# Experts of a sparse feed-forward block: tiles of 128 rows against 544 slots per expert in two column phases

## The chip, the cores and the metric

The kernel runs on one core of one Trainium2 chip. The metric is device time in microseconds, the median of three runs. TensorE is written PE in the profile (PEld for its weight loads), VectorE DVE, ScalarE ACT, GpSimd POOL, SyncE SP.

## The reference

The input x has 4 images of 512 channels on 16 x 32 positions. A layer norm over channels, a causal depthwise convolution along the channel axis with 3, 7 and 15 taps, a 96-to-32 mixing and a residual come first. The change is in what follows, on 2048 tokens of 512 features:

```python
t = _to_tokens(x)                       # 2048 tokens x 512
xn = _ln_t(t)
probs = softmax(xn @ gate_w.T)          # 8 experts
topk_w, topk_idx = top_k(probs, 2); topk_w /= topk_w.sum(-1)
h = silu(xn @ w1[e]) * (xn @ w3[e])     # 512 -> 1024, every expert e
y = h @ w2[e]                           # 1024 -> 512
t = t + sum_e y_e * full_w[:, e]
```

The kernel computes each expert only for the tokens that chose it, 4096 pairs of token and expert. The result must hold float32 accuracy, so each product of matrices is made from a high part (float32r, written hi) and a low part (lo, the rest): hi x hi, lo x hi and hi x lo, three matmuls.

## The kernel before

**Ahead of the experts.** The convolution stage ends with the normalised tokens in DRAM (xn_rows), the gate logits, and the residual sums in the output. DVE finds two experts per token, ranks tokens within each expert and builds one-hot matrices; slots(0) and slots(1) (L671) multiply them, and bank 5 then holds the token number of each slot, 16 columns of 128 slots per expert. From it come src_i (what to gather), dst_i (where to add) and gate_i (which gate).

**Tiles.** An expert's slots are worked in tiles of 128 rows, only as many as its tokens need; DVE computes a table of live tiles (tile_expert, tile_last, tile_col), and every engine runs a loop over up to 39 tiles with values loaded from it. 36 tiles are live here.

**One tile on TensorE** (pe_tile). The stationary operand is always 128 x 128 of the rows (xT_hi, xT_lo, hT_hi, hT_lo), the moving one 512 columns of weights. up(k) for four units of w1 and w3 is 4 x 12 products; turn_h transposes h (L734), turn_tokens the next tile's gathered rows (L712), 12 transposes together; down sums 24 products into bank 7. ACT applies silu (L559), makes high parts (L563, L572) and writes y scaled by the gate (L580). DVE multiplies (L1042) and makes low parts (L1046, L1019).

**Weights.** Each expert has six units of 128 x 2048 (1 MB). SP loads unit k of the next expert when its low half is made; ACT makes the high half (high_half, L265), DVE the low half (low_half, L270), POOL that of unit 1. This is done in an expert's last tile.

**POOL's queue** (pool_tile) is strictly in program order. In a tile it gathers the rows of the tile after next, as soon as xg is free (after turn_tokens), and then waits for y:

```python
next_expert(1)
pool.wait_ge(xg_ps, t2)                       # gather, L404
...
pool.wait_ge(y_out, t1)                       # then y's rows: add_at, gate_at
pool.indirect_dma_start(out=out, ..., in_=y[:], compute_op=ALU.add)   # L438
gather_gates(gate_at[:, 0:1])                 # L410
```

y is one buffer: ACT waits for the add to have landed (y_st) before it writes the next. SP waits at L333 until all adds have landed.

**Columns of the rows.** In a row such as `437.00 0.18 POOL L428 COPY gather_at<-src_i`, the first number is the start in us from the span's start, the second the length.

Of the kernel before, what the change touches and what calls it, by code (L numbers as in the profile page):

```python
# [6 lines left out]
F32R = mybir.dt.float32r  # L7
I32 = mybir.dt.int32
ALU = mybir.AluOpType
# [20 lines left out]
TILES = NT * 2 + E - 1  # L30
SLOT_TILES = 2 * -(-(TILES + 2) // 2)
# [9 lines left out]
GRID = TOKENS // P  # L41

# [67 lines left out]
def metaformer(nc, xt, taps_d, mix_d, joint_d, gate_d, units, out):  # L110

    with ExitStack() as ctx:
# [37 lines left out]
        xg = at("xg", XT_AT, [P, NQ, P])  # L150
        y = at("y", XT_AT + 2 * KB, [P, L])

        hT_hi = at("hT_hi", F_AT, [P, 2, 4, P], F32R)
        hT_lo = at("hT_lo", F_AT + 4 * KB, [P, 2, 4, P], F32R)
        xT_hi = at("xT_hi", F_AT + 8 * KB, [P, NQ, P], F32R)
        xT_lo = at("xT_lo", F_AT + 10 * KB, [P, NQ, P], F32R)
        h = at("h", F_AT + 12 * KB, [P, 2, 512])
        xnb = [at(f"xnb{n}", F_AT + 2 * KB * n, [P, NB, P]) for n in range(XB)]
        h_at = F_AT + 12 * KB
        over = at("over", h_at, [P, E, GRID])  # L160
        passed = at("passed", h_at + 512, [P, SLOT_TILES, E])
        te = at("te", h_at + 1856, [P, 4, SLOT_TILES])
        number, empty = (at(n, h_at + 2560 + 512 * k, [P, P]) for k, n in enumerate(("number", "empty")))
# [3 lines left out]
        def keep(name, shape, dt=F32):  # L167

            size = 4
            for n in shape[1:]:  # L170
# [17 lines left out]
        slot_gate = keep("slot_gate", [P, SLOT_TILES])  # L188
        gather_at = keep("gather_at", [P, 1], I32)
        add_at = keep("add_at", [P, 1], I32)  # L190
        gate_at = keep("gate_at", [P, 1], I32)
        gate_row = keep("gate_row", [P, 1])
        tile_col = keep("tile_col", [1, SLOT_TILES], I32)
        tile_expert = keep("tile_expert", [1, TILES], I32)
        tile_last = keep("tile_last", [1, TILES], I32)
        all_tiles = keep("all_tiles", [1, 1], I32)
# [49 lines left out]
        gates_made, gate_st, gate_index, gate_land = (sem("gates_made"), sem("gate_st"), sem("gate_index"),  # L246
                                                      sem("gate_land"))
        xn_half, scanned = sem("xn_half"), sem("scanned")
        src_ready, tables_ready, gate_ready = sem("src_ready"), sem("tables_ready"), sem("gate_ready")
# [3 lines left out]
        xg_in, xg_ps, xT_hi_out, xT_lo_out = sem("xg_in"), sem("xg_ps"), sem("xT_hi_out"), sem("xT_lo_out")  # L253
        unit_done = sem("unit_done")
        silu_out, h_out, hT_ps, hT_hi_out, hT_lo_out = (sem("silu_out"), sem("h_out"), sem("hT_ps"),
                                                        sem("hT_hi_out"), sem("hT_lo_out"))
        y_out, y_st = sem("y_out"), sem("y_st")
# [17 lines left out]
        def _(sp):  # L275
# [54 lines left out]
            sp.wait_ge(tables_ready, 1)  # L330
            total = sp.value_load(all_tiles[0:1, 0:1], min_val=E, max_val=TILES)
            sp.wait_ge(y_st, total * 16)
# [3 lines left out]
        def _(pool):  # L336
# [65 lines left out]
            def gather(index):  # L402

                pool.indirect_dma_start(  # L404
                    out=xg[:].rearrange("p q i -> p (q i)"), out_offset=None, in_=xn_dram,
                    in_offset=bass.IndirectOffsetOnAxis(ap=index, axis=0)).then_inc(xg_in, 16)

            def gather_gates(index):

                pool.indirect_dma_start(  # L410
                    out=gate_row[:], out_offset=None, in_=gate_dram,
                    in_offset=bass.IndirectOffsetOnAxis(ap=index, axis=0)).then_inc(gate_land, 16)

            def column(t):
                return pool.value_load(tile_col[0:1, bass.ds(t, 1)], min_val=0, max_val=P - 1)

            def pool_tile(t, t1, t2, following):

                last = pool.value_load(tile_last[0:1, bass.ds(t, 1)], min_val=0, max_val=1)

                def next_expert(k):

                    with pool.If_ne(last.val, 0):
                        low_half(pool, following, k)

                next_expert(1)
                pool.wait_ge(xg_ps, t2)
                pool.tensor_copy(gather_at[:], src_i[:, bass.ds(column(t2), 1)]).then_inc(gather_index, 1)  # L428
                pool.wait_ge(xn_st[XB - 1], 16 * NT // XB)
                pool.wait_ge(gather_index, t2)  # L430
                gather(gather_at[:, 0:1])

                pool.wait_ge(y_out, t1)
                pool.tensor_copy(add_at[:], dst_i[:, bass.ds(column(t), 1)]).then_inc(add_index, 1)  # L434
                pool.tensor_copy(gate_at[:], gate_i[:, bass.ds(column(t1), 1)]).then_inc(gate_index, 1)  # L435
                pool.wait_ge(spare_st, 16)
                pool.wait_ge(add_index, t1)
                pool.indirect_dma_start(  # L438
                    out=out, out_offset=bass.IndirectOffsetOnAxis(ap=add_at[:, 0:1], axis=0),
                    in_=y[:], in_offset=None, compute_op=ALU.add).then_inc(y_st, 16)  # L440
                pool.wait_ge(gate_st, 16)
                pool.wait_ge(gate_index, t1)
                gather_gates(gate_at[:, 0:1])
# [6 lines left out]
            gather(src_i[:, 0:1])  # L450
            pool.wait_ge(tables_ready, 1)
            pool.wait_ge(gate_st, 16)
            gather_gates(gate_i[:, 0:1])
            pool.wait_ge(xg_ps, 1)
            pool.tensor_copy(gather_at[:], src_i[:, bass.ds(column(1), 1)]).then_inc(gather_index, 1)
            pool.wait_ge(gather_index, 1)
            gather(gather_at[:, 0:1])
            pool_tile(0, 1, 2, 1)
            with pool.Fori(1, TILES) as t:
                live = pool.value_load(tile_expert[0:1, bass.ds(t, 1)], min_val=0, max_val=E)  # L460
                with pool.If_ne(live.val, 0):
                    pool_tile(t, pool.snap(t + 1), pool.snap(t + 2), live)
                    pool.nop()

        @block.scalar
        def _(act):
# [69 lines left out]
            for k in range(3):  # L536
                high_half(act, 0, k)

            act.wait_ge(ex_in, 1)
            act.activation(ex[:], ex[:], ACT.Exp).then_inc(ex_out, 1)  # L540

            act.wait_ge(xg_ps, 1)
            act.activation(xT_hi[:], B[6][:].rearrange("p (q i) -> p q i", i=P), ACT.Copy).then_inc(xT_hi_out, 1)
            for k in range(3, UNITS):
                high_half(act, 0, k)

            def act_tile(t, following):
                last = act.value_load(tile_last[0:1, bass.ds(t, 1)], min_val=0, max_val=1)

                def next_expert(*ks):  # L550

                    with act.If_ne(last.val, 0):
                        for k in ks:
                            act.wait_ge(unit_done, t * UNITS + (k + 1))
                            high_half(act, following, k)

                def silu(j):
                    act.wait_ge(unit_done, t * UNITS + (2 * j + 1))
                    act.activation(h[:, j, :], B[2 * j][:], ACT.Silu).then_inc(silu_out, 1)  # L559

                def hi(j):
                    act.wait_ge(hT_ps, t * 2 + (j + 1))
                    act.activation(hT_hi[:, j, :, :], B[4 + j][:].rearrange("p (c n) -> p c n", n=P),  # L563
                                   ACT.Copy).then_inc(hT_hi_out, 1)

                silu(0)
                next_expert(0, 1)
                silu(1)
                hi(0)
                next_expert(2)  # L570
                act.wait_ge(xg_ps, t + 2)
                act.activation(xT_hi[:], B[6][:].rearrange("p (q i) -> p q i", i=P),  # L572
                               ACT.Copy).then_inc(xT_hi_out, 1)
                hi(1)
                next_expert(3, 4)
                act.wait_ge(unit_done, t * UNITS + UNITS)
                act.wait_ge(gate_ready, t + 1)
                if not isinstance(t, int):
                    act.wait_ge(y_st, t * 16)
                act.activation(y[:].rearrange("p (q i) -> p q i", i=P), B[7][:].rearrange("p (i q) -> p q i", q=NQ),  # L580
                               ACT.Copy, scale=slot_gate[:, bass.ds(t, 1)]).then_inc(y_out, 1)

                next_expert(5)

            act.wait_ge(tables_ready, 1)
            act_tile(0, 1)
            with act.Fori(1, TILES) as t:
                live = act.value_load(tile_expert[0:1, bass.ds(t, 1)], min_val=0, max_val=E)
# [545 lines left out]
```

## Time and profile before

| | |
|---|---|
| three runs | 847.27, 848.59, 849.71 us, median 848.59 |
| profiled execution | 847.05 us, of it span 845.4 us |
| PE / DVE / ACT / POOL busy | 94 / 42 / 38 / 32% |
| granted TensorE clock, mean over the span | 0.97 |
| chain that ended last | PE 86%, DVE 7%, DMA 2% |

The chain of work that ended last is followed back from the last instruction; 86% of it is TensorE. TensorE's busy time comes from modelled ends of pipelined matmuls, so intervals between starts say more than lengths do.

### The profile page before, as it was taken

How to read it: one execution, taken by the hardware profiler on the slowest of the kernel's cores; microseconds unless marked ns; L12 is line 12 of the kernel's file. 1: busy time of each engine (PE TensorE's matmuls, PEld its weight loads, DVE VectorE, ACT ScalarE, POOL GpSimd, SP SyncE). 2: the span in 40 equal slices, each digit the busy share in tenths (PEclk: the TensorE clock that was granted, in tenths of full speed). 3: DMA queues.
4: the chain of work that ended last, by engine and by line, in shares of the span. 5: the costliest groups of instructions: out<-in, count | busy, mean ns of one | idle time of the engine just before them, and what ended most of it. 6: DMA issues, size and time to landing. Idle time of an engine off the chain costs nothing.

```text
span 845.4 us, 13004 instructions
## 1 busy us (share of the span) xinstructions
PE 791.5 (94%) x3764; PEld 655.6 (78%) x3765; DVE 351.7 (42%) x791; ACT 318.6 (38%) x487; POOL 268.8 (32%) x313
## 2 busy tenths in 40 slices
PE   4999999628999999999999999999999999999993
PEld 3777888527888888888888888888888888888882
DVE  5886758685113621172216223511361172244111
ACT  6784755432214512262127125311441262262120
POOL 4346210003233422361216315322341262243311
PEclk9999999659999999999999999999999999999997
DMA  7247678628111811173116513712281164111111
GB/s 237 47 75 138 150 162 175 256 105 326 25 31 34 317 39 25 27 263 95 32 30 201 159 25 88 271 25 37 46 302 37 25 224 136 25 37 25 30 32 25
DMA packets 55873, 91.72 MB, mean 108 GB/s; under 512 B 7344, under 2 KB 40496, under 8 KB 49712
## 3 DMA queue, kind: packets, MB, share of 16 engines
q1 hardware_dynamic: 45728, 71.64, 27.2%
q0 software_dynamic: 9408, 19.42, 12.0%
q10 hardware_dynamic: 720, 0.46, 0.2%
q8 instruction: 7, 0.11, 0.1%
q14 instruction: 10, 0.08, 0.0%
HBM read 64.97 MB, written 18.15 MB: 98 GB/s over the span
## 4 chain that ended last, share of the span: by engine, by line
PE 86%; DVE 7%; DMA 2%; issue 2%; ACT 1%; POOL 0%; POOLq 0%; ACTq 0%; DVEq 0%
PE bank L720 23%; PE bank L718 23%; PE bank L719 23%; PE bank L734 4%; PE bank L631 3%; PE bank L632 3%; PE bank L633 3%; PE bank L712 2%; PE bank L653 1%; DMA xg<-xn_rows,gather_at 1%; DVE bn L782 1%; DVE wc_lo L823 1%; PE bank L671 1%; PE bank L646 1%; DVE mv L791 1%
## 5 line engine op out<-in xcount | busy, mean ns | idle before, releaser
L718 PE MATMUL bank<-w_hi,xT_hi 128*128 128x512 f32 x576 | 229.0, 398 | 4.3 <-DVE xT_lo L1019 4.3
L720 PE MATMUL bank<-w_hi,xT_lo 128*128 128x512 f32 x576 | 225.9, 392 | 0.0
L719 PE MATMUL bank<-w_lo,xT_hi 128*128 128x512 f32 x576 | 225.2, 391 | 0.0
L1042 DVE TENSOR_TENSOR h<-bank,h 128x512 f32<-128x512 f32 x72 | 49.8, 692 | 294.0 <-PE bank L720 293.8
L718 PEld LDWEIGHTS bank<-w_hi,xT_hi 128*128 128x128 f32 x576 | 108.9, 189 | 26.3 <-DVE xT_lo L1019 4.7
L720 PEld LDWEIGHTS bank<-w_hi,xT_lo 128*128 128x128 f32 x576 | 108.7, 189 | 23.4
L719 PEld LDWEIGHTS bank<-w_lo,xT_hi 128*128 128x128 f32 x576 | 108.9, 189 | 21.8
L718 PE MATMUL bank<-w_hi,hT_hi 128*128 128x512 f32 x288 | 118.7, 412 | 0.0
L559 ACT ACTIVATE h<-bank 128x512 f32<-128x512 f32 x72 | 43.1, 599 | 197.4 <-PE bank L720 197.4
L720 PE MATMUL bank<-w_hi,hT_lo 128*128 128x512 f32 x288 | 112.6, 391 | 0.0
L719 PE MATMUL bank<-w_lo,hT_hi 128*128 128x512 f32 x288 | 112.3, 390 | 0.0
L1046 DVE TENSOR_TENSOR hT_lo<-bank,hT_hi 128x512 fp32r<-128x512 f32 x72 | 49.8, 692 | 112.7 <-ACT hT_hi L563 112.7
L265 ACT ACTIVATE w_hi<-w_raw 128x2048 fp32r<-128x2048 f32 x48 | 90.8, 1911 | 8.4 <-DMA w_raw<-in_units 6.2
L270 DVE TENSOR_TENSOR w_lo<-w_raw,w_hi 128x2048 fp32r<-128x2048 f32 x41 | 91.6, 2282 | 0.0
L580 ACT ACTIVATE y<-bank,slot_gate 128x512 f32<-128x512 f32 x36 | 24.8, 690 | 134.0 <-PE bank L720 134.0
L434 POOL COPY add_at<-dst_i 128x1 int32 x36 | 16.0, 444 | 177.5 <-ACT y L580 177.5
L372 POOL TENSOR_TENSOR wc<-taps,mixT 128x256 f32<-128x256 f32 (+4 forms) x48 | 41.7, 888 | 74.5 <-DVE wc_lo L823 71.8
L438 POOL DMA_INDIRECT out_x<-y,add_at x36 | 58.5, 1625 | 19.5 <-POOL gate_at L435 17.8
L720 PEld LDWEIGHTS bank<-w_hi,hT_lo 128*128 128x128 f32 x288 | 54.1, 188 | 11.8
L719 PEld LDWEIGHTS bank<-w_lo,hT_hi 128*128 128x128 f32 x288 | 54.4, 189 | 8.7
L631 PE MATMUL bank<-xs_parts,wc_hi 128*128 128x512 f32 x128 | 54.8, 428 | 6.6 <-DVE xs_parts L817 6.6
L718 PEld LDWEIGHTS bank<-w_hi,hT_hi 128*128 128x128 f32 x288 | 54.2, 188 | 8.6
(145 smaller groups left out, 924.2 us busy)
## 6 DMA issues: line engine op xcount, KB each, us to landing
w_raw<-in_units SPq DMA_DIRECT2D x48, 1024.0 KB, 5.9
joint<-xs_parts SPq DMA_DIRECT2D x64, 128.0 KB, 3.8
out_x<-XT SPq DMA_DIRECT2D x17, 256.0 KB, 3.6
XT<-in_x SPq DMA_DIRECT2D x16, 256.0 KB, 7.0
xn_rows<-xnb SPq DMA_DIRECT2D x16, 256.0 KB, 2.5
xg<-xn_rows,gather_at POOLq DMA_INDIRECT x37, 3.4
out_x<-y,add_at POOLq DMA_INDIRECT x36
gate_row<-gate_rows,gate_at POOLq DMA_INDIRECT x36
```

The costliest lines, as they stand in the source:

```text
L265: eng.activation(w_hi[k][:], w_raw[k][:], ACT.Copy).then_inc(hi_ready[k], 1)
L270: eng.tensor_tensor(w_lo[k][:], w_raw[k][:], w_hi[k][:], ALU.subtract).then_inc(lo_ready[k], 1)
L372: ins = pool.tensor_tensor(wc[t % WB][:, at_col:at_col + count * P].rearrange("p (a d q) -> p a d q", d=D, q=NQ), lags.rearrange("p (a q) ...
L438: pool.indirect_dma_start(out=out, out_offset=bass.IndirectOffsetOnAxis(ap=add_at[:, 0:1], axis=0), in_=y[:], in_offset=None, compute_op=A ...
L559: act.activation(h[:, j, :], B[2 * j][:], ACT.Silu).then_inc(silu_out, 1)
L631: pe.matmul(out_bank, wc_hi[t % WB][:, cols], hi, start=first, stop=False)
L718: pe.matmul(B[bank][:], stat_hi, hi, start=start, stop=False)
L719: pe.matmul(B[bank][:], stat_hi, lo, start=False, stop=False)
L720: return pe.matmul(B[bank][:], stat_lo, hi, start=False, stop=stop)
L734: ins = pe.transpose(B[4 + j][:, P * c:P * c + P], h[:, j, P * c:P * c + P], ident[:])
L1042: dve.tensor_tensor(h[:, j, :], B[2 * j + 1][:], h[:, j, :], ALU.mult).then_inc(h_out, 1)
L1046: dve.tensor_tensor(hT_lo[:, j, :, :], B[4 + j][:].rearrange("p (c n) -> p c n", n=P), hT_hi[:, j, :, :], ALU.subtract).then_inc(hT_lo_out, 1)
```

## The change

The loop over tiles goes. Each expert has 4 x 128 + 32 = 544 slots (ROOM), worked without conditions in two phases: wide, with 128 + 128 + 32 = 288 slots, and even, with 128 + 128 = 256. Expert 0 and expert 7 are written out, 1 to 6 are a loop. A loop for leftover tiles of experts with more than 544 tokens stands at the end (rest_live, rest_expert, rest_col).

- First products (up): the weights are stationary, 128 x 128 of them, and the slots' columns move, 288 or 256. A chunk c of eight is 128 hidden features, 24 products into two banks. h comes out already transposed, and turn_h is gone.
- ACT and DVE work per chunk on 288 or 256 columns: silu, product, high part, low part.
- Second products (down_rows): the rows stay stationary, 512 columns of w2 move, one sum per tile: three sums after the wide phase (128, 128 and 32 rows), two after the even one. w2's columns are laid out in another order on the host.
- Two buffers for gathered rows, five for gates; y stays one buffer.
- The gather of tile 3 stands first in pool_expert, that of tile 4 next; then tiles 0 and 1 of the next expert, then the adds.
- POOL makes no low halves any more. DVE's table of leftovers, slot tables and gates move into expert 0. count(1) runs ahead of slots(0); all six high halves of expert 0 are made ahead of its x.

```diff
+ROOM = 4 * P + P // 4
+WIDE, EVEN = 2 * P + P // 4, 2 * P
+TILE = ((0, 0, 0, P), (1, 0, P, P), (4, 0, 2 * P, P // 4), (2, 1, 0, P), (3, 1, P, P))
...
+            def gather_tile(column, m, buffer, turned, nth):
+
+                pool.wait_ge(xt_ps, nth)
+                pool.wait_ge(xt_ps, turned)
+                pool.tensor_copy(gather_at[buffer][:], src_i[:, bass.ds(pool.snap(column), 1)]).then_inc(gather_index, 1)
+                pool.wait_ge(src_ready, 1)
+                pool.wait_ge(gather_index, nth)
+                gather(xg[buffer][0:m], gather_at[buffer][0:m, 0:1], xg_in[buffer])
+
+            def add_rows(column, m, nth):
+
+                pool.wait_ge(y_out, nth)
+                pool.tensor_copy(add_at[:], dst_i[:, bass.ds(pool.snap(column), 1)]).then_inc(add_index, 1)
...
+            def pool_expert(e, first=False, last=False):
+
+                def gather_next(j, buffer, ahead, turned, nth):
+                    gather_tile(e * GRID + (GRID * ahead + TILE[j][0]), TILE[j][3], buffer, e * 5 + turned, e * 5 + nth)
+
+                def add(j):
+                    add_rows(e * GRID + TILE[j][0], TILE[j][3], e * 5 + (j + 1))
+                    if not last:
+                        next_gates(j, e * GRID + (GRID + TILE[j][0]), e * 5 + (j + 1))
+
+                gather_next(3, 1, 0, 2, 1)
+                gather_next(4, 0, 0, 3, 2)
...
+                if not last:
+                    gather_next(0, 0, 1, 5, 3)
+                    gather_next(1, 1, 1, 5, 4)
+                for j in range(3):
+                    add(j)
+                if not last:
+                    gather_next(2, 0, 1, 6, 5)
+                for j in range(3, len(TILE)):
+                    add(j)
...
+            def chunk(c, n, cols, opening=False):
+                act.wait_ge(up_ps, n(c + 1))
+                if not opening:
+                    act.wait_ge(hT_lo_out, n(c - 1))
+                act.activation(hs[c % 2][:, 0:cols], B[2 * (c % 2)][:, 0:cols], ACT.Silu).then_inc(silu_out, 1)
+                act.wait_ge(h_out, n(c + 1))
+                act.activation(hT_hi[:, c, 0:cols], hs[c % 2][:, 0:cols], ACT.Copy).then_inc(hT_hi_out, 1)
+
+            def rows_out(j, bank, m, nth, gates, opening=False):
+                act.wait_ge(y_ps, nth + 1)
+                act.wait_ge(gate_land[j], gates)
+                if not opening:
+                    act.wait_ge(y_st, nth * 16)
+                act.activation(y[0:m], B[bank][0:m, :], ACT.Copy, scale=slot_gate[0:m, j:j + 1]).then_inc(y_out, 1)
...
+                for j, bank in enumerate((4, 6, 7)):
+                    tile_rows(j, bank)
+                for c in range(HC):
+                    chunk(c, even, EVEN)
+                    if c in (1, 3, 5) and not last:
+                        x_high(c // 2, 5, e * 5 + (6 + c // 2))
+                    if c in (4, 6) and not last:
+                        if c == 4:
+                            act.wait_ge(up_ps, even(4))
+                        high_half(act, e + 1, (c - 4) // 2)
+                if not last:
+                    act.wait_ge(up_ps, even(8))
+                    high_half(act, e + 1, 2)
+                    high_half(act, e + 1, 3)
+                tile_rows(3, 4)
+                tile_rows(4, 6)
...
+            def up(c, n, cols, i, split, opening=False):
...
+                if not opening:
+                    pe.wait_ge(h_out, n(c - 1))
+                at_col = slice(P * (c % 4), P * (c % 4) + P)
+                for m in range(2):
+                    k, hidden = c // 4 * 2 + m, B[2 * (c % 2) + m][:, 0:cols]
+                    for a in range(NQ):
+                        x_hi, x_lo = xT_hi[i][:, a, 0:cols], xT_lo[i][:, a, 0:cols]
+                        pe.matmul(hidden, w_hi[k][:, a, at_col], x_hi, start=(a == 0), stop=False)
+                        pe.matmul(hidden, w_lo[k][:, a, at_col], x_hi, start=False, stop=False)
+                        ins = pe.matmul(hidden, w_hi[k][:, a, at_col], x_lo, start=False, stop=(a == NQ - 1))
+                ins.then_inc(up_ps, 1)
+
+            def down_waits(c, n, split):
+
+                if c % 4 == 0:
+                    pe.wait_ge(lo_ready[4 + c // 4], split)
+                if c == 0:
+                    pe.wait_ge(hT_lo_out, n(HC - 1))
+                if c == HC - 1:
+                    pe.wait_ge(hT_lo_out, n(HC))
+
+            def down_rows(first, bank, n, split, m=P):
+
+                for c in range(HC):
+                    down_waits(c, n, split)
+                    k, a = 4 + c // 4, c % 4
+                    hi, lo = hT_hi[:, c, first:first + m], hT_lo[:, c, first:first + m]
+                    pe.matmul(B[bank][0:m, :], hi, w_hi[k][:, a, :], start=(c == 0), stop=False)
+                    pe.matmul(B[bank][0:m, :], hi, w_lo[k][:, a, :], start=False, stop=False)
+                    ins = pe.matmul(B[bank][0:m, :], lo, w_hi[k][:, a, :], start=False, stop=(c == HC - 1))
+                ins.then_inc(y_ps, 1)
...
+                for c in range(HC):
+                    if c == 0:
+                        pe.wait_ge(xT_lo_out, e * 5 + 3)
+                    up(c, wide, WIDE, 0, split, first and c < 2)
+                    if c == 1:
+                        gathered(1, e * 32 + 32, 3)
+                        turn_x(xg[1], 5, P)
+                    if c == 4:
+                        gathered(0, e * 48 + 32, 4)
+                        turn_x(xg[0], 5, P)
...
+                for c in range(HC):
+                    if c == 0:
+                        pe.wait_ge(xT_lo_out, e * 5 + 5)
+                    if not last and c == 5:
+                        gathered(0, e * 48 + 64, 7)
+                    up(c, even, EVEN, 1, split)
...
+                for c in range(HC):
+                    chunk(c, even, EVEN)
+                    if c in (1, 3, 5) and not last:
+                        x_low_half(c // 2, 5, e * 5 + (6 + c // 2))
+                    if c in (5, 7) and not last:
+                        low_half(dve, e + 1, (c - 5) // 2)
+                if not last:
+                    low_half(dve, e + 1, 2)
+                    low_half(dve, e + 1, 3)
```

In the diff, functions with pool. stand on POOL, act. on ACT, pe. on TensorE, dve. on DVE; the last piece is dve_expert's even phase. The wait in gathered(1, ...) is for the landed gather of tile 3.

## Rows read from the trace of the kernel before

**Rows 1.** The page: the span, then busy time of each engine

```profile
span 845.4 us, 13004 instructions
...
PE 791.5 (94%) x3764; PEld 655.6 (78%) x3765; DVE 351.7 (42%) x791; ACT 318.6 (38%) x487; POOL 268.8 (32%) x313
```

**Rows 2.** Windows: stretch and length, busy time (count) by engine, granted clock, DMA

```profile
core 0: us, PE busy (x) PEld busy (x) DVE busy (x) ACT busy (x) POOL busy (x), PEclk, DMA share, GB/s
...
147.50:153.00 5.50, 3.33 (x28) 2.91 (x26) 3.79 (x17) 3.71 (x10) 0.00 (x0) 1.00 0.32 95
...
158.70:188.60 29.90, 11.31 (x51) 10.53 (x50) 24.35 (x78) 9.77 (x8) 1.14 (x1) 0.50 0.53 217
188.60:194.00 5.40, 5.33 (x13) 4.17 (x14) 5.30 (x7) 4.72 (x3) 0.19 (x1) 0.50 0.50 112
194.00:200.00 6.00, 6.00 (x30) 4.99 (x29) 5.15 (x4) 0.91 (x2) 5.13 (x3) 0.99 1.00 412
```

**Rows 3.** Timeline of TensorE's weight loads (PEld), at both clocks: start, length

```profile
189.69 0.33 PEld L718 LDWEIGHTS bank<-w_hi,xT_hi 128*128 128x128 f32 x1
...
190.12 0.33 PEld L719 LDWEIGHTS bank<-w_lo,xT_hi 128*128 128x128 f32 x1
...
264.42 0.19 PEld L718 LDWEIGHTS bank<-w_hi,xT_hi 128*128 128x128 f32 x1
...
269.86 0.19 PEld L718 LDWEIGHTS bank<-w_hi,xT_hi 128*128 128x128 f32 x1
```

**Rows 4.** Timeline of TensorE around four transposes of h

```profile
272.35 0.19 PEld L720 LDWEIGHTS bank<-w_hi,xT_lo 128*128 128x128 f32 x1
...
272.81 0.60 PE L734 MATMUL bank<-ident,h 128*128 128x128 f32 x4
...
273.48 0.19 PEld L720 LDWEIGHTS bank<-w_hi,xT_lo 128*128 128x128 f32 x1
```

**Rows 5.** Groups of instructions: count, busy us, mean ns, idle before and its releaser

```profile
L718 PE MATMUL bank<-w_hi,xT_hi 128*128 128x512 f32 x576 | 229.0, 398 | 4.3 <-DVE xT_lo L1019 4.3
...
L718 PE MATMUL bank<-w_hi,hT_hi 128*128 128x512 f32 x288 | 118.7, 412 | 0.0
...
L270 DVE TENSOR_TENSOR w_lo<-w_raw,w_hi 128x2048 fp32r<-128x2048 f32 x41 | 91.6, 2282 | 0.0
L265 ACT ACTIVATE w_hi<-w_raw 128x2048 fp32r<-128x2048 f32 x48 | 90.8, 1911 | 8.4 <-DMA w_raw<-in_units 6.2 <-PE bank L720 2.2
...
L559 ACT ACTIVATE h<-bank 128x512 f32<-128x512 f32 x72 | 43.1, 599 | 197.4 <-PE bank L720 197.4
```

**Rows 6.** Timeline from the first gather to the first product

```profile
179.64 1.14 POOL L404 DMA_INDIRECT xg<-xn_rows,src_i  x1 [51.66 <-DVE src_i L975]
...
188.67 0.79 PE L718 MATMUL bank<-w_hi,xT_hi 128*128 128x512 f32 x1 [4.29 <-DVE xT_lo L1019]
```

**Rows 7.** Timeline of the end: last product, y, its rows added

```profile
831.90 0.39 PE L720 MATMUL bank<-w_hi,hT_lo 128*128 128x512 f32 x1
832.57 0.69 ACT L580 ACTIVATE y<-bank,slot_gate 128x512 f32<-128x512 f32 x1 [4.44 <-PE bank L720]
...
835.56 1.62 POOL L438 DMA_INDIRECT out_x<-y,add_at  x1 [0.60 <-POOL gate_at L435]
```

**Rows 8.** SP's last wait, which ends when all rows are added: last start

```profile
L333 SPq EVENT_SEMAPHORE  x1: 17/17/17, 840.2 to 840.2; - x1
```

**Rows 9.** Timeline of POOL, one gather of token rows

```profile
437.00 0.18 POOL L428 COPY gather_at<-src_i 128x1 int32 x1 [6.38 <-PE bank L712]
437.94 0.97 POOL L404 DMA_INDIRECT xg<-xn_rows,gather_at  x1 [0.76 <-POOL gather_at L428]
```

**Rows 10.** Timeline: a gather's issue on POOL while DVE makes weight halves

```profile
191.87 6.69 DVE L270 TENSOR_TENSOR w_lo<-w_raw,w_hi 128x2048 fp32r<-128x2048 f32 x3
...
196.66 2.74 POOL L404 DMA_INDIRECT xg<-xn_rows,gather_at  x1 [0.27 <-POOL gather_at L455]
```

**Rows 11.** Gathers of token rows, all 38: from issue to landing

```profile
DMA to landing us min/median/max: 3.1/3.4/8.3
```

More of the change, by code:

```diff
@@ L29 @@
 E = 8
-TILES = NT * 2 + E - 1
-SLOT_TILES = 2 * -(-(TILES + 2) // 2)
 UNITS = 6
@@ L400, in _, with gather @@
                 multiply_taps(t)
[L402 removed]
+            def gather(out_rows, index, landed):
                 pool.indirect_dma_start(
[L405 to L408 removed]
+                    out=out_rows.rearrange("p q i -> p (q i)"), out_offset=None, in_=xn_dram,
+                    in_offset=bass.IndirectOffsetOnAxis(ap=index, axis=0)).then_inc(landed, 16)
@@ L410, in gather_gates @@
+            def gather_gates(j, index):
+                m = TILE[j][3]
                 pool.indirect_dma_start(
[L411 to L435, printed above, removed]
@@ L534, in _ @@
                     wc_high(t + 2)
-            for k in range(3):
+            for k in range(UNITS):
                 high_half(act, 0, k)
[L539 to L572, printed above, removed]
-                               ACT.Copy).then_inc(xT_hi_out, 1)
[L574 to L583, printed above, removed]
@@ new lines, in _ @@
+            pe.wait_ge(src_ready, 2)
+            pe.wait_ge(xg_in[0], 16)
+            turn_x(xg[0], 5, P)
+            pe.wait_ge(xg_in[1], 16)
+            turn_x(xg[1], 4, P)
+            pe.wait_ge(xg_first, 16)
+            turn_x(y_rows, 6, P // 4)
+            pe_expert(0, first=True)
+            with pe.Fori(1, E - 1) as e:
+                pe_expert(e)
+            pe_expert(E - 1, last=True)
+            pe.wait_ge(rest_ready, 1)
+            total = pe.value_load(all_rest[0:1, 0:1], min_val=0, max_val=REST)
@@ L982, in _ @@
-            then_next(dve.tensor_tensor(upto[:], upto_e[:], ntile[:].unsqueeze(1).broadcast_to([P, E, E]), ALU.mult))
-            then_next(dve.tensor_reduce(end[:], upto[:], AX_X, ALU.add))
-            slots_by_e = [1, SLOT_TILES, E]
-            ends = end[0:1, :].unsqueeze(1).broadcast_to(slots_by_e)
-            expert, live, following, column = (te[0:1, k, :] for k in range(4))
-            then_next(dve.tensor_tensor(passed[0:1], iota[0:1, 0:SLOT_TILES].unsqueeze(2).broadcast_to(slots_by_e),
-                                        ends, ALU.is_ge))
@@ new lines, in dve_expert, with wide, even @@
+            def dve_expert(e, first=False, last=False):
+                def wide(c):
+                    return e * 16 + c
+                def even(c):
+                    return e * 16 + (8 + c)
+                for c in range(HC):
+                    chunk(c, wide, WIDE)
+                    if first and c < 2:
+                        low_half(dve, 0, 2 + c)
+                    if c == 1:
+                        x_low_half(3, 5, e * 5 + 4)
+                    if first and c == 2:
+                        gate_shifts()
+                        slot_tables()
+                    if first and c == 3:
+                        make_gates()
+                    if c == 4:
+                        x_low_half(4, 5, e * 5 + 5)
+                    if c in ((4, 5) if first else (1, 3)):
+                        low_half(dve, e, 4 + (c - 4 if first else c // 2))
+                    if first and c == 6:
+                        rest_tables()
+                for c in range(HC):
+                    chunk(c, even, EVEN)
[6 more added lines that the diff above has]
+                    low_half(dve, e + 1, 3)
@@ new lines, in _ @@
+            for j, bank in enumerate((5, 4, 6)):
+                x_low_half(j, bank, j + 1)
+            dve_expert(0, first=True)
+            with dve.Fori(1, E - 1) as e:
+                dve_expert(e)
+            dve_expert(E - 1, last=True)
+            dve.wait_ge(rest_ready, 1)
+            everything = dve.value_load(all_rest[0:1, 0:1], min_val=0, max_val=REST)
+            with dve.If_ne(everything.val, 0):
+                with dve.Fori(0, REST) as r:
+                    live = dve.value_load(rest_live[0:1, bass.ds(r, 1)], min_val=0, max_val=1)
+                    with dve.If_ne(live.val, 0):
+                        x_low_half(0, 5, r + (E * len(TILE) + 1))
+                        for k in range(UNITS):
+                            low_half(dve, r + E, k)
+                        for c in range(HC):
+                            chunk(c, lambda k: r * 8 + (16 * E + k), P)
+                        dve.nop()
```

405 lines of the change are left out of this document (226 added, 179 removed).

## The prediction, made before the run

> **What bounds the kernel now.** Three views. The page gives a span of 845.4 us with TensorE busy for 94% of it [rows 1]; the execution took 847.05 us, 1.5 under the median of 848.59. The windows split it [rows 2]: until 158.7 the convolution, until 188.6 a thin stretch at half clock with TensorE busy for 11 of 30 us, then the experts with it always busy. The experts begin at 188.67 [rows 6] and their last product starts at 831.90 [rows 7], 643.4 us with its own 0.23. The timeline prices a product: its load and its 512 columns come every (269.86 - 264.42)/24 = 0.227 us at full clock, 0.43 at half [rows 3]. The reader is to see 512 columns at 2.4 GHz, 0.213, plus 0.014. Around four transposes three products take 1.13 us instead of 0.68 [rows 4]: 0.45 for four, 0.11 for a pair of load and 128 columns, twice what 128 columns need. So a load alone costs about 0.11, hidden under 512 columns and not under 128. Counting: 3 x 576 first and 3 x 288 second products [rows 5], 2592 in all, by 0.227 are 588.4, and 36 tiles with 12 transposes are 108 groups by 0.45, 48.6. Together 637.0 of 643.4; half clock until 194.0 [rows 2] explains 2.5 of the rest. The stage is TensorE's stream, without waits. What the change does to that stream, and to what it waits for, decides.
>
> **The stream after.** The reference's own inputs give 487 to 534 tokens per expert, so all fit in 544 slots and the tail for leftovers stays empty. First products: per expert 192 with 288 columns and 192 with 256. Second products: five sums by 24, 120 with 512 columns; the sum for 32 rows costs as much as one for 128. Columns are the same as before: 8 x (192 x 544 + 120 x 512) = 1,327,104 = 2592 x 512. The transposes of h go; those of x are 40 groups of four, 40 x 0.45 = 18.0. The gain is 30.6 us of transposes; the loss is that 2592 products become 8 x 504 = 4032 shorter ones. What a pair costs at 288 and 256 columns no row shows. Below: the larger of the columns (0.120, 0.107) and a load (about 0.11), so 0.120 and 0.108. With the 0.014 of rows 3 as a fixed part per pair: 0.1335 and 0.1202; with it in proportion, 0.1276 and 0.1134. Worse is possible, since load and columns are now equally long: I bound it by 0.150 for both, half way from the columns alone to load plus columns. I take the middle of fixed and proportional, 0.1305 and 0.117. Stream: 1536 x 0.1305 + 1536 x 0.117 + 960 x 0.227 + 18.0 = 200.4 + 179.7 + 217.9 + 18.0 = 616.0, that is 21 less than 637.0.
>
> The Trainium skill ("TensorE: Matmul & The Clock Gate", Back-to-back issue gap) gives N/2.4 + 2.5 ns per product at full clock, 0.1225 and 0.109 here; by it the sum below would end near 886. Its LDWEIGHTS section gives columns/1.2, 107 ns for 128: that agrees with the 0.11 of rows 4 and speaks against 256 columns, which no longer cover a load with anything to spare. At 512 columns its first rule gives 0.216 where rows 3 show 0.227, so I hold to the rows.
>
> **The new wait.** The order on POOL matters most. pool_expert(e) begins with the gather of tile 3 of its own expert, behind the last add and the last gate gather of expert e-1 in program order. TensorE wants this tile after two chunks of the wide phase. Before, the gather stood ahead of y's add and had a whole tile of some 17 us. From F, the first even second product:
>
> - TensorE: two sums, 48 x 0.227 = 10.9, then two chunks, 48 x 0.1305 = 6.3. It asks at F+17.2.
> - Tile 3's sum ends at F+5.4; ACT starts y 0.67 after the last product's start [rows 7], F+5.9, but two high halves of 1.91 [rows 5] stand before it, until about F+6.5. y is written by F+7.2.
> - POOL: copy 0.2, then 0.76 to the DMA instruction [rows 9]: F+8.4. DVE makes three low halves of 2.28 [rows 5] in F+3.1 to F+9.9, and a POOL issue beside such work took 2.74 instead of 0.97 [rows 10]. The add lands 4.6 after issue if undisturbed (835.56 to 840.2 [rows 7, 8]); here the next weights load at once, and a gather landed in up to 8.3 instead of 3.4 [rows 11] while the DMA share was 1.00 [rows 2]. I take 7: F+15.4.
> - y is one buffer, so tile 4's y waits for that landing: F+16.3 written. Copy and issue: F+17.4; 1.62 for the add [rows 7]; copy, 0.76, 0.99 for the gates: F+21.0; copy and 0.76: the gather issues at F+22.1 and lands 3.4 later [rows 11], F+25.5.
>
> TensorE waits 8.3 us in each of seven experts (the first has its gather early): 58. Without DVE's and the loads' disturbance and the high halves it is 5.2, so 36; with all of them in full 9.9, so 69. Nothing can be gained here.
>
> After such a gap the clock is likely low. In rows 2 it was granted in full until 153.0, though work thinned from 147.5, was half by 153, and came back only 5.4 us into the dense work of 188.6. 5.4 us at half clock give 5.4 x (1 - 0.1305/0.24) = 2.5 less work: seven times 17, from 0 (no fall) to 24.
>
> **Smaller terms.** The even second products wait for h's low part of chunk 6, which stands on DVE behind a low half of 2.28 begun after chunk 5: about 0.7 late, seven times 5 (0 to 10). The tile-2 gather of the next expert is asked for after five even chunks and lands at about the same time, cost 0 to 1 each; it is late next if products are quicker. Chunks: silu 0.4, product 0.4, copy 0.4, low part 0.4, estimates from 0.60 for 512 columns on ACT [rows 5], lie inside the 3.1 and 2.8 us of TensorE's next chunk. Gate and table arithmetic on DVE moves from before the first product into expert 0, with two table switches on ACT: hidden mostly, 1 us. What it frees at the start is used up: three gathers 1.4 apart from 179.64 [rows 6] land the last at 186.1, and turning and splitting it ends near 188.3, so the first product starts as now. count(1) ahead of slots(0) fills an idle stretch. POOL's low halves go to DVE, beside slack. The end: y 4 waits 0.7 for y 3, while POOL saves a column load and a copy, 0.
>
> **Sum.** 616.0 + 6.4 of other time as now + 58 + 17 + 5 + 1 = 703.4 against 643.4: 60 more. 847.05 + 60 = 907.
>
> **Rivals.**
> - *Faster.* The gather is in time. For it: POOL is busy only 32% [rows 1], and the gather's operands are ready a phase earlier. Against: POOL's program order puts it behind y of tile 4, which exists only at F+11 even without any wait, and rows 7, 9 and 11 leave at least 0.2 + 0.76 + 1.62 + 1.9 + 1.0 + 3.4 = 8.9 behind it. It decides if the landing comes before F+17.2, 8.3 earlier than I sum. Time: 907 - 58 - 17 = 832.
> - *The clock stays up* through the gaps: 907 - 17 = 890. For it: in rows 2 it held through 5.5 us with TensorE busy for 3.3. Against: here the gap is empty and longer.
> - *Pairs at their lower bound*: only the 6 wide and 8 even chunks outside the gap count, (144 x 0.0105 + 192 x 0.009) x 8 = 26 less: 881.
> - *Loads not hidden*, 0.150: (144 x 0.0195 + 192 x 0.033) x 8 = 73 more: 980.
> - *The change does not do what it says*: an expert over 544 tokens would reload all weights for a leftover tile. The counts exclude it.
>
> **How the numbers follow.** My forecast 57%, clock kept 18%, lower bound 12%, loads not hidden 5%, faster 7%, no change 1%. What a measurement can tell from no change is about 0.3%, 2.5 us. Faster 0.07, same 0.02, slower 0.91. The forecast's own range, gap 36 to 69, clock 0 to 24, pairs -26 to +8, mostly independent: 880 to 934. The range 868 to 938 leaves out the faster case and the unhidden loads, and takes in two favourable bounds together.
>
> **What would show it.** Per expert from 2 to 8, one idle stretch of 5 to 10 us on TensorE, ended by the gather of tile 3, after the second wide chunk, and half clock behind it; weight loads every 0.13 and 0.12 us in the first products; an execution of even second products that starts some 0.7 us late. Wrong would be: no such stretch (then 832), a pair over 0.14, or a second wait of the same size, above all ACT held by y in front of the even chunks, or the tile-2 gather.

## The result, and the profile after

The changed kernel takes 913.11 us, median of 4 runs (912.6 to 914.46), the kernel before 847.93 beside it: 7.69% slower, ratio 1.0769, interval 1.0746 to 1.0792. The profiled execution has a span of 911.0 us. The forecast was 907, with a range of 868 to 938.

The page of the changed kernel: span, busy time by engine, granted clock in 40 slices, the chain that ended last.

```profile
span 911.0 us, 13256 instructions
...
PE 797.7 (88%) x4928; PEld 711.1 (78%) x4929; DVE 373.6 (41%) x876; ACT 337.5 (37%) x607; POOL 233.8 (26%) x318
...
PEclk9999998579997999799979997999799979998997
...
PE 70%; DMA 10%; DVE 8%; issue 5%; POOL 4%; ACT 3%; POOLq 0%; ACTq 0%; DVEq 0%
```

Against [rows 1] TensorE's busy time has grown by 6 us and its share has fallen from 94 to 88%: the time came as waiting. The clock row has a dip in every fourth slice from the 13th to the 37th, which the kernel before had nowhere in its expert stage, and the chain holds 10% of DMA where it held 2%.

Who waited for whom, on TensorE in the expert stage: total us, times, longest.

```profile
PE bank L785 <- DMA xg<-xn_rows,gather_at: 62.1, 7, 9.8
...
PE bank L820 <- DVE hT_lo L1172: 1.1, 1, 1.1
```

Seven stretches, one for each expert from the second on, all ended by a gather. L785 is turn_x. The next rows are windows of one of them, the second expert's: start:end and length, busy time (count) by engine, granted clock, DMA.

```profile
core 0: us, PE busy (x) PEld busy (x) DVE busy (x) ACT busy (x) POOL busy (x), PEclk, DMA share, GB/s
259.00:270.00 11.00, 11.00 (x50) 8.91 (x49) 7.46 (x5) 5.76 (x6) 3.33 (x3) 1.00 0.66 258
270.00:276.50 6.50, 6.50 (x50) 6.44 (x48) 0.02 (x1) 0.99 (x2) 1.19 (x2) 1.00 0.72 226
276.50:285.00 8.50, 0.22 (x2) 0.00 (x0) 1.81 (x4) 2.98 (x4) 5.21 (x7) 0.73 0.34 62
285.00:290.50 5.50, 5.38 (x23) 5.39 (x24) 2.89 (x2) 0.60 (x1) 0.00 (x0) 0.50 0.17 51
290.50:297.60 7.10, 7.10 (x55) 7.10 (x54) 2.91 (x5) 3.52 (x5) 0.00 (x0) 0.99 0.40 148
```

The even second products (259.0 to 270.2), two wide chunks, then 8.5 us of nothing, then 5.5 us at half clock. (A PEclk of 0.73 or 0.69 is a mean over a stretch in which the clock went from full to half.) These windows are the forecast's F to F+38. What lies in the gap is read from the chain that ended last, in order of time, over the same stretch (start, length, what; TensorE's own pieces and the short ones between are left out):

```profile
264.80 0.70 ACT y L602
265.55 0.31 POOL add_at L439
265.90 0.76 issue
266.66 8.69 DMA out_x<-y,add_at
275.46 0.70 ACT y L602
276.21 0.20 POOL add_at L439
276.45 0.75 issue
277.20 1.61 POOL out_x L442
278.81 0.21 POOL gate_at L449
279.06 0.49 issue
279.91 0.88 issue
280.78 0.23 POOL gather_at L431
281.06 0.50 issue
281.76 3.31 DMA xg<-xn_rows,gather_at
```

With F = 259.02 this is the chain of the forecast step by step: y of tile 3 at F+5.8 (5.9 without the high halves, 6.5 with them forecast), its add issued at F+7.6 (8.4), landed at F+16.3 (15.4), tile 4's add issued at F+18.2 (17.4), the gather at F+22.7 (22.1), landed at F+26.1 (25.5). TensorE's last product before it starts at F+17.4, so by the spacing TensorE asks at F+17.5 (17.2).

This stretch is not like the other six. The same chain in the third expert's (F = 348.78) and in the eighth's (F = 800.21), and between them what DVE did in the third's:

```profile
355.48 2.34 POOL add_at L439
358.63 7.24 DMA out_x<-y,add_at
...
351.08 6.69 DVE L273 TENSOR_TENSOR w_lo<-w_raw,w_hi 128x2048 fp32r<-128x2048 f32 x3
...
810.06 4.92 DMA out_x<-y,add_at
```

In experts 3 to 8 POOL's copy of one column into add_at takes 2.34 instead of 0.31, and it ends 0.05 behind the last of DVE's three low halves. So the add is issued at F+9.8 (8.4 forecast), and tile 4's y starts at F+16.9 to F+17.7 in experts 3 to 7. In the eighth, which has no next weights to load, the add lands in 4.92 and y starts at F+14.8. By the starts, the stretches are 8.6, 9.3, 10.0, 9.4, 9.7, 9.3 and 7.0 us.

The products themselves, as weight loads of the changed kernel: start, length, line.

```profile
290.59 0.19 PEld L802 LDWEIGHTS bank<-xT_lo,w_hi 128*128 128x128 f32 x1
...
291.92 0.19 PEld L800 LDWEIGHTS bank<-xT_hi,w_hi 128*128 128x128 f32 x1
...
246.87 0.19 PEld L800 LDWEIGHTS bank<-xT_hi,w_hi 128*128 128x128 f32 x1
...
252.48 0.19 PEld L802 LDWEIGHTS bank<-xT_lo,w_hi 128*128 128x128 f32 x1
```

Ten loads in 1.33 us in the wide phase, 0.133 each; 47 in 5.61 in the even one, 0.119. That is columns plus 0.013 in both, the fixed form of the 0.014 of [rows 3].

### The profile page after: what moved, and what is told of

Same layout as the page of the kernel before. It is cut to its first block, busy times and chain, and to the rows that moved or that the text cites. A ratio compares the mean times of both kernels' runs of the same rounds, so it can differ in the third digit from the quotient of the medians.

```text
span 911.0 us, 13256 instructions
## 1 busy us (share of the span) xinstructions
PE 797.7 (88%) x4928; PEld 711.1 (78%) x4929; DVE 373.6 (41%) x876; ACT 337.5 (37%) x607; POOL 233.8 (26%) x318
## 4 chain that ended last, share of the span: by engine, by line
PE 70%; DMA 10%; DVE 8%; issue 5%; POOL 4%; ACT 3%; POOLq 0%; ACTq 0%; DVEq 0%
PE bank L800 13%; PE bank L801 12%; PE bank L802 12%; PE bank L820 7%; PE bank L822 7%; PE bank L821 6%; DMA out_x<-y,add_at 6%; PE bank L705 3%; DMA xg<-xn_rows,gather_at 3%; PE bank L706 2%; PE bank L707 2%; PE bank L785 2%; POOL add_at L439 2%; POOL out_x L442 1%; PE bank L727 1%
## 5 line engine op out<-in xcount | busy, mean ns | idle before, releaser
L800 PE MATMUL bank<-xT_hi,w_hi 128*128 128x256 f32 (+1 forms) x1024 | 306.3, 299 | 1.0 <-DVE xT_lo L1164 1.0
L801 PE MATMUL bank<-xT_hi,w_lo 128*128 128x256 f32 (+1 forms) x1024 | 302.0, 295 | 0.0
L802 PE MATMUL bank<-xT_lo,w_hi 128*128 128x256 f32 (+1 forms) x1024 | 301.3, 294 | 0.0
L800 PEld LDWEIGHTS bank<-xT_hi,w_hi 128*128 128x128 f32 x1024 | 200.2, 196 | 2.7 <-DVE xT_lo L1164 1.2
L801 PEld LDWEIGHTS bank<-xT_hi,w_lo 128*128 128x128 f32 x1024 | 200.0, 195 | 0.6
L802 PEld LDWEIGHTS bank<-xT_lo,w_hi 128*128 128x128 f32 x1024 | 199.8, 195 | 0.0
L820 PE MATMUL bank<-w_hi,hT_hi 128*128 128x512 f32 (+1 forms) x320 | 126.6, 396 | 1.3 <-DVE hT_lo L1172 1.1
L822 PE MATMUL bank<-w_hi,hT_lo 128*128 128x512 f32 (+1 forms) x320 | 125.9, 394 | 0.0
L821 PE MATMUL bank<-w_lo,hT_hi 128*128 128x512 f32 (+1 forms) x320 | 125.5, 392 | 0.0
L785 PE MATMUL bank<-ident,xg 128*128 128x128 f32 (+1 forms) x156 | 26.8, 301 | 68.8 <-DMA xg<-xn_rows,gather_at 62.1
L1172 DVE TENSOR_TENSOR hT_lo<-hs,hT_hi 128x256 fp32r<-128x256 f32 (+1 forms) x128 | 56.6, 443 | 63.7 <-ACT hT_hi L595 63.2
L785 PEld LDWEIGHTS bank<-ident,xg 128*128 128x128 f32 (+1 forms) x156 | 19.6, 157 | 71.9 <-DMA xg<-xn_rows,gather_at 56.7
```

The lines of the kernel that those rows point to most:

```text
L785: ins = pe.transpose(B[bank][:, m * q:m * q + m], buffer[0:m, q, :], ident[0:m, 0:m])
L800: pe.matmul(hidden, w_hi[k][:, a, at_col], x_hi, start=(a == 0), stop=False)
L801: pe.matmul(hidden, w_lo[k][:, a, at_col], x_hi, start=False, stop=False)
L802: ins = pe.matmul(hidden, w_hi[k][:, a, at_col], x_lo, start=False, stop=(a == NQ - 1))
L820: pe.matmul(B[bank][0:m, :], hi, w_hi[k][:, a, :], start=(c == 0), stop=False)
L821: pe.matmul(B[bank][0:m, :], hi, w_lo[k][:, a, :], start=False, stop=False)
```

## The experiments

Seven kernels. Each is the changed kernel with the edit shown, unless said otherwise. A period is the time from one expert's even second products to the next's, by the timeline; in the changed kernel it is 90.2 us on average over the first six.

**The early gathers.**

```diff
             def pool_expert(e, first=False, last=False):
...
-                gather_next(3, 1, 0, 2, 1)
-                gather_next(4, 0, 0, 3, 2)
                 if first:
+                    gather_next(3, 1, 0, 2, 1)
+                    gather_next(4, 0, 0, 3, 2)
...
                     gather_next(2, 0, 1, 6, 5)
+                    gather_next(3, 1, 1, 7, 6)
+                    gather_next(4, 0, 1, 8, 7)
                 for j in range(3, len(TILE)):
```

> The changed kernel with one move on POOL: the gathers of tiles 3 and 4 of the next expert are issued behind that of its tile 2, ahead of the last two adds, as soon as TensorE has turned what lay in their buffers. Theory (the wait is POOL's program order): the seven idle stretches of 6.9 to 9.8 us on TensorE, 62 in all, go, and with them the seven falls of the clock, 5.4 us of dense work at half clock each, worth 2.4 each, 17 in all. 913 - 62 - 17 = 834 us, against 848 for the kernel before. Rival A: a wait just behind takes the place (ACT held by y's add in front of the even chunks, or the gather of tile 4): some stretches of 2 to 5 us stay and the time is 850 to 880. Rival B: the stretches come from the gather itself, slow in the DMA queues: they stay at 8 us, 913.

846.88 us, ratio to the kernel before 0.999 (0.9981 to 1.0). The gather waits are gone from the list, the clock stays full from 191 us to the end, and the period is 80.6. 66 of the 79 expected us came back. The rest is rival A in small: a new entry in the waits on TensorE, and ACT's timeline beside it.

```profile
PE bank L802 <- DVE hs L1171: 8.3, 12, 1.0
```

```profile
276.08 0.69 ACT L604 ACTIVATE y<-bank,slot_gate 128x512 f32<-128x512 f32 x1 [10.98 <-DMA out_x<-y,add_at]
276.66 0.40 ACT L595 ACTIVATE hs<-bank 128x288 f32<-128x288 f32 x1
277.59 0.44 ACT L597 ACTIVATE hT_hi<-hs 128x288 fp32r<-128x288 f32 x1 [0.52 <-DVE hs L1171]
277.94 1.90 ACT L268 ACTIVATE w_hi<-w_raw 128x2048 fp32r<-128x2048 f32 x1
```

ACT stood 10.98 us before y of tile 4, until tile 3's rows had landed, and only then made the silu of the first wide chunk, which TensorE's third chunk needs. Two stretches near 1 us each, 1.9 by the starts, in each of the experts 2 to 7. The eighth has none: there tile 3's rows landed earlier, with no loads beside them. The sum expected below for both edits together counts seven times 2.0; six times 1.9 are 11.5 us.

**Filler on TensorE.**

```diff
                     if c == 1:
+                        if not first:
+                            for _ in range(38):
+                                pe.matmul(B[7][:], w_hi[0][:, 0, 0:P], w_hi[0][:, 1, :], start=True, stop=True)
                         gathered(1, e * 32 + 32, 3)
```

> The changed kernel with 38 added products of 512 columns into bank 7 (free then) on TensorE after the second wide chunk of experts 2 to 8, ahead of its wait for tile 3; nothing reads them. They take 38 x 0.227 = 8.6 us, about as long as the idle stretch, and do no useful work. Theory (the fall of the clock costs 17 us by itself): the clock stays full in the expert stage, the stretch is filled, and the time is 896, from 893 to 900. Rival: the clock costs nothing that the pipeline doesn't get back: 913 or more, since the filler overshoots the gather in the shortest stretch (6.9) by 1.7.

902.75 us (899.47 to 902.9), ratio 1.0648 (1.063 to 1.0666), 10.4 under the changed kernel, where 893 to 900 was expected; the profiled execution, the fastest of the four, has a span 13.4 under it. A window through the filler and one behind it:

```profile
270.00:290.00 20.00, 19.77 (x117) 17.54 (x116) 3.37 (x6) 4.58 (x7) 7.63 (x11) 1.00 0.51 144
290.00:360.00 70.00, 70.00 (x460) 62.65 (x459) 26.75 (x38) 24.61 (x41) 16.47 (x21) 1.00 0.31 95
```

Behind the stretch, the four transposes of tile 3 and the third to fifth chunk, from the first start to the last: first in the changed kernel, then with the filler.

```profile
285.12 1.11 PE L785 MATMUL bank<-ident,xg 128*128 128x128 f32 x4 [8.40 <-DMA xg<-xn_rows,gather_at]
...
297.52 0.29 PE L802 MATMUL bank<-xT_lo,w_hi 128*128 128x288 f32 x1
...
287.14 0.66 PE L785 MATMUL bank<-ident,xg 128*128 128x128 f32 x4 [0.23 <-DMA xg<-xn_rows,gather_at]
...
297.08 0.30 PE L802 MATMUL bank<-xT_lo,w_hi 128*128 128x288 f32 x1
```

The clock is 1.00 throughout and the period is 87.8, 2.4 shorter with TensorE doing 38 useless products in it. Not all of the 2.4 is the clock. The same work behind the stretch takes 12.4 us in the changed kernel and 9.9 with the filler; over the seven stretches the difference is between 1.7 and 2.6, 14.9 in all, 2.1 on average. The stretches themselves, from the product ahead to the first transpose, sum to 64.2 us in both kernels. So the fall of the clock has a price of its own, 14.9 us, where 17 was expected. The profile closes with it: the first expert's even second products, ahead of any filler, begin 1.5 us later (0.6 of it ahead of the stage), and 14.9 - 1.5 is the 13.4. Why they do, and why the three other executions took 3 us more than the profiled one, isn't settled.

**Two buffers for y.**

```diff
+        y = [at("y0", xg_at + 4 * KB, [P, L]), at("y1", hs_at + 8 * WIDE, [P, L])]
...
             def rows_out(j, bank, m, nth, gates, opening=False, waits=(), b=0):
...
-                if not opening:
-                    act.wait_ge(y_st, nth * 16)
-                act.activation(y[0:m], B[bank][0:m, :], ...)
+                for buffer, landed in waits:
+                    act.wait_ge(y_st[buffer], landed * 16)
+                act.activation(y[b][0:m], B[bank][0:m, :], ...)
```

Tile 0 still waits for all adds, since a token may be in two experts; add_at is doubled too.

> The changed kernel with two buffers for y (and for add_at), each with its own semaphore of landed adds: the y of tile 4 no longer waits for the rows of tile 3 to have landed. The order on POOL is as in the changed kernel. By the chain from the first even second product (F): y of tile 4 is written at F+12.0 instead of F+17.1, its add issues at F+13.4, behind the gates of tile 3, instead of F+18.2, the gather lands at F+21.3 instead of F+26.1. Theory: each stretch is 4.8 us shorter, 3.8 instead of 8.6: 34 less, 879; if the clock no longer falls in them, 17 less again, 862. Rival (y's single buffer is not in the chain; POOL is simply late with its queue): no change, 913.

880.02 us, ratio 1.0379 (1.0362 to 1.0396), 33 less. Waits on TensorE, and windows from the third expert:

```profile
PE bank L795 <- DMA xg<-xn_rows,gather_at: 34.6, 7, 5.3
```

```profile
361.50:366.50 5.00, 0.02 (x1) 0.00 (x0) 0.92 (x2) 0.91 (x3) 3.19 (x5) 1.00 0.36 83
366.50:372.00 5.50, 5.30 (x29) 5.30 (x30) 2.89 (x2) 0.60 (x1) 0.00 (x0) 0.69 0.17 48
```

The stretches go from 62.1 to 34.6, 3.9 less each where 4.8 was expected. The 4.8 was read from the second expert's chain, and there 4.7 came; in the others POOL's held copy (2.33 us) keeps the next add back too. The clock now falls only as the stretch ends and is back within 3.5 us, so part of its price returns: the work behind the stretches takes 10 us more than with the filler, where it was 14.9. y's single buffer is in the chain.

**Later loads.**

```diff
             with sp.Fori(2, E) as e:
                 for k in range(UNITS):
                     sp.wait_ge(lo_ready[k], e)
+                    if k == 1:
+                        sp.wait_ge(y_st, e * 80 - 80)
                     load_unit(e, k)
```

Expert 1's loads are written out ahead of the loop, without the wait.

> The changed kernel with one wait added on SP: units 1 to 5 of the expert after next are loaded only when all adds of the expert at hand have landed, so no weights are on the DMA engines while the rows of tile 3 are added. Theory (the add of tile 3 landed 8.8 us after its issue, against 4.6 undisturbed, since three loads of 1 MB ran beside it): it lands in 5 to 6 us, each stretch is 3 to 4 us shorter, and the time is 885 to 893. Rival (the add is late because DVE's low halves hold up POOL's issue of it, 2.8 instead of 1.6 us): at most 1 us for each expert, 906 to 913.

917.16 us, ratio 1.0827 (1.0804 to 1.0851), 4 more: neither of the two expected. The chain over the same stretch says why.

```profile
266.94 6.04 DMA out_x<-y,add_at
...
279.69 7.14 DMA xg<-xn_rows,gather_at
```

The add of tile 3 takes 6.04 instead of 8.69, as the theory wants, with POOL's issue held as before (2.83). But the loads are let go as the last add lands, at 279.86, 0.17 behind the issue of the gather, and the gather takes 7.14 instead of 3.31. The contention was moved, not removed. Both terms are shown: three loads of 1 MB make an add of rows 2.7 later or a gather 3.8 in the stretch shown, 2.3 to 3.0 and 2.2 to 3.8 over experts 2 to 7. The eighth expert, which has no loads, has its add in 4.9 and its gather in 3.4 in both kernels.

**Early gathers and two buffers.** Both diffs above together.

> Both edits of the first runs at once: the early gathers of tiles 3 and 4, and two buffers for y. With the early gathers alone an expert took 80.6 us and TensorE still stood for two short stretches of the wide phase, 1.1 behind the turning of tile 3 and about 0.9 behind the fourth chunk, since ACT was held by y of tile 4 until the rows of tile 3 had landed, and so was late with silu of the first wide chunks. Theory: y's second buffer frees ACT, both stretches go, an expert takes 78.6 us, and the time is 846.9 - 7 x 2.0 = 833, 1.7% under the kernel before. Rival (the stretches come from the high halves on ACT or low halves on DVE in these chunks): they stay, 845 to 847.

833.65 us (833.58 to 834.62, 5 runs), ratio to the kernel before 0.9841 (0.9827 to 0.9855): 1.6% faster, as expected (833). Every period is 78.68 us. The window over six experts, beside [rows 2]:

```profile
360.00:800.00 440.00, 440.00 (x2931) 398.20 (x2930) 163.68 (x238) 158.83 (x265) 119.04 (x156) 1.00 0.31 89
```

**The gathers between the last two adds.**

```diff
-                for j in range(3, len(TILE)):
-                    add(j)
+                add(3)
+                if not last:
+                    gather_next(3, 1, 1, 7, 6)
+                    gather_next(4, 0, 1, 8, 7)
+                add(4)
```

The two at the head of pool_expert are for expert 0 only, as with the early gathers.

> The changed kernel with the gathers of tiles 3 and 4 moved ahead of the last add only, behind the add and the gates of tile 3. By the changed kernel's trace POOL is free then at F+12.5, so the gather issues at F+13.5 and lands at F+16.9 undisturbed, before TensorE asks at F+17.5. Theory (the price is in y of tile 4 and its add, in front of the gather): no idle stretch or one under 2 us, and the same 1.1 and 0.9 us as with the early gathers, 847 to 855; nearer 870 if the three weight loads then on the DMA engines delay the gather, as an add was delayed by 4. Rival (any place behind an add is as late as the present one): over 890.

846.19 us, ratio 0.9988 (0.9979 to 0.9997). The gather waits are 2.2 us in all, 0.6 the longest. Moving the gather past one add and one gate gather is worth as much as moving it past both; the wait for y of tile 4 was the price. The held copy shows here too: the gather is issued at F+13.4 in the second expert, as expected, and at F+14.4 in the others, so it lands a little after TensorE asks.

**Narrower products.**

```diff
-                    k, hidden = c // 4 * 2 + m, B[2 * (c % 2) + m][:, 0:cols]
+                    k, hidden = c // 4 * 2 + m, B[2 * (c % 2) + m][:, 0:{WIDE: 224, EVEN: 192, P: P}[cols]]
                     for a in range(NQ):
-                        x_hi, x_lo = xT_hi[i][:, a, 0:cols], xT_lo[i][:, a, 0:cols]
+                        n_cols = {WIDE: 224, EVEN: 192, P: P}[cols]
+                        x_hi, x_lo = xT_hi[i][:, a, 0:n_cols], xT_lo[i][:, a, 0:n_cols]
```

> A measurement of the pair of weight load and moving columns, not a full computation: the changed kernel with 224 instead of 288 columns in the first products of the wide phase and 192 instead of 256 in the even one, on TensorE alone; the last 64 slots of each phase are left out of the first products. In the changed kernel a pair comes every 0.133 us with 288 columns and 0.120 with 256, columns plus 0.0135 each time. Theory A (columns plus a fixed part, and never under the 0.109 of a load): 0.109 to 0.110 with 224 and the same with 192. Theory B (at 256 the load already binds, at 0.107 plus a fixed 0.013): 0.120 with both. The time has no other meaning; by A the first products shrink by about 26 us outside the idle stretches.

One run, 883.78 us, for the pair alone: the kernel leaves out the last 64 slots of each phase, so its time has no other meaning. In the wide phase, loads of this kernel:

```profile
296.49 0.19 PEld L801 LDWEIGHTS bank<-xT_hi,w_hi 128*128 128x128 f32 x1
...
304.53 0.19 PEld L821 LDWEIGHTS bank<-w_hi,hT_hi 128*128 128x128 f32 x1
```

72 pairs in 8.04 us, 0.112 each; the even phase has 0.111 with 192 columns. Theory A: at 192 and 224 columns the pair no longer follows the columns, and what is left in it is the load, about 0.11; at 256 and 288 it is the columns plus 0.013. Where between 224 and 256 the two meet no run shows. B's 0.120 is excluded.

## Why the prediction was right, by its steps

The expert stage lasted 643.4 us and lasts 710.0 (187.98 to 897.98); 703.4 was forecast. Term by term:

| term | forecast | measured |
|---|---|---|
| 1536 products of 288 columns | 200.4 | 204.3 (0.133) |
| 1536 of 256 | 179.7 | 183.5 (0.1195) |
| 960 second products | 217.9 | 222.5 (0.2318) |
| 40 groups of transposes | 18.0 | 14 (37 of them in the stage) |
| seven gather waits | 58 | 62.1 |
| clock behind them | 17 | 15 (2.1 each) |
| even second products late | 5 | 0 |
| first expert, other | 7.4 | 8.6, what is left |

The last row is the stage less the others: 710.0 - 701.4. That the sum is only 6.6 us short is partly luck: the stream is 8 too low and the wait 4, and 5 for the even second products and 2 for the clock are too high.

- **The stream** was right in kind. Between fixed and proportional I took the middle; the fixed form was right, 8 us more, and the rival at the lower bound (881) is out. The second products cost 0.232 instead of 0.227 with the same shapes, 5 more. The kernel before has this spacing too, in the products just behind transposes (nine in 2.08 us from 255.97 on, 0.231 each, and 0.227 each from 261.9); no run says why. The transposes among short products cost 0.36 for four, not 0.45.
- **The new wait** was in the place, of the length and for the reason given. Early gathers removed it, the gather between the adds removed it, two buffers shortened it: POOL's program order with y's single buffer in front of it is shown, and the faster rival with 832 us is what the kernel becomes when both are mended (833.65). That the rival's 832 is met so closely is luck as well, since it holds the same wrong terms. The mis-sized step lies between tile 3's y and the y of tile 4, and two terms share it. In the second expert it is "I take 7" for the landing of tile 3's add: 8.8 from issue to the y behind it, 2.7 of it the weights on the DMA engines, by the later loads, and 1.2 in POOL's issue of it, which took 2.83 instead of 1.61. In experts 3 to 8 it is the term ahead, "copy 0.2": the copy took 2.34 and the add was issued at F+9.8 instead of F+8.4, and from there 7 was right (7.1 to 7.9 to the y, 4.9 in the eighth). Issue and copy are long only beside DVE's low halves, and the copy ends with them; no run takes the low halves away. One miss hid part of it: "two high halves ... stand before it, until about F+6.5" (ACT was free at F+5.5).
- **The clock** fell in each stretch, at 280.3 in the one shown, and was back 5.5 us into dense work, as [rows 2] had it at 188.6; over the seven stretches that is 3.7 to 5.7. The filler shows the price alone. The rival with 890 is out.
- **The even second products late by 0.7** did not happen: the last product of the even chunks and the first second product are 0.12 apart in experts 2 to 8. The low half did stand in front of chunk 6 on DVE (254.89 to 257.17 in the second expert), but chunk 6's low part was made by 258.43, 0.6 before the first second product: the step was 1.3 too pessimistic. Only the first expert has 1.1 us, before its wide second products.
- **The rival with loads not hidden** (980) is out at 0.133 and 0.1195, and the narrow products show how near it was: at 256 columns the moving part, 0.107 + 0.013, is only 0.009 above the load's 0.11. The bound of 0.150 was also not the half way it was called, which is 0.175 and 0.162 by its own terms; the measured pairs lie under all of them. By the Trainium skill ("TensorE: Matmul & The Clock Gate", Back-to-back issue gap) a matmul by itself takes 0.109 and 0.1225 here, and the section says that this has no room for a weight load; both measurements are 0.010 above it. The Trainium skill's section LDWEIGHTS on the same page gives columns/1.2, 107 ns for 128; the 0.111 and 0.112 agree with it to 5 ns.

What the change is worth without its wait: 833.65 against 847.17 beside it, 13.5 us, 11.1 of it in the expert stage (643.4 to 632.3). The rows give nearly that: transposes go from 48.6 us (the forecast's sum for the kernel before) to 14, 34.6 less, and products from 588.4 to 204.3 + 183.5 + 222.5 = 610.3, 21.9 more: 12.7.

## What to carry to other kernels

When a loop is rewritten, write down the program order of the slowest queue and ask of every gather in it what stands ahead: an operand that is ready a phase early is of no use behind a wait for the last result. A single buffer between an engine and a DMA turns the DMA's landing into part of both engines' queues; here one more 256 KB buffer was worth 33 us before the order was mended and 13 after. A wait of several microseconds on TensorE can cost more than it lasts, by the clock: here seven of 8.9 us on average cost 2.1 more each. And read every instance of a repeated stretch, not the first alone: here the copy that held up six of the seven was short in the one read first.

## What the runs showed of the hardware

- A pair of float32r load and product takes the columns at 2.4 GHz plus 0.013 us at 256, 288 and 512 columns, but never under 0.111 (192 and 224 columns alike).
- The clock fell within a stretch of 8.4 idle us and even at the end of one of 5.2, and a stretch of at most 1.1 us never brought it down.
- Beside three weight loads an indirect add of 128 rows lands 2.7 us later, and a gather of 128 rows 3.8.
- A POOL indirect issue beside DVE's 2048-column low halves took 2.83 instead of 1.61 us, as the gather of [rows 10] did.
